# Spectra of the later rows as full-precision products instead of split ones, in a fused decoder-layer kernel

## The reference, cut to what matters

```
x = x + autocorrelation(Q = layernorm(x), K = ctx, V = ctx)

qf, kf = fft(q), fft(k)                      # over the 128 tokens, for each feature
corr   = ifft(qf * conj(kf)).real
w, idx = top_k(corr over the tokens, 9 of 128)
w      = softmax(w)
out    = sum over i of w_i * v shifted by idx_i   (positions clamped at the last token)
```

## Time and profile before

| | before |
|---|---|
| median of 3 runs | 1228.88 us (1228.21 to 1229.78) |
| profiled execution | 1230.26 us, span 1228.4 us |
| TensorE busy | 1022.5 us (83%) |
| VectorE busy | 929.4 us (76%) |
| ScalarE busy | 610.1 us (50%) |
| GpSimd busy | 486.6 us (40%) |
| mean granted TensorE clock | 0.927 |

### The profile page before, as it was taken

How to read it: one execution, slowest core, us unless ns; L and a number is a source line. 1 busy time by engine, 2 the same in 40 slices (tenths; PEclk the granted TensorE clock), 3 DMA queues, 4 the chain that set the end, 5 groups by cost and what they waited for, 6 DMA issues and landing times. The chain is left out here.

```text
span 1228.4 us, 23475 instructions
## 1 busy us (share of the span) xinstructions
PE 1022.5 (83%) x7936; PEld 776.0 (63%) x7936; DVE 929.4 (76%) x2818; ACT 610.1 (50%) x1803; POOL 486.6 (40%) x676
## 2 busy tenths in 40 slices
PE   5699999999999999999657999999898787615056
PEld 4577777877777777777445677777666564313034
DVE  6766786666787666776604878879999999997994
ACT  6434555444555544555515667777565564212023
POOL 2523433333443333443313766666565563101020
PEclk9799999999999999999778999999999998857579
DMA  9011011111011111011122222422332211139025
GB/s 378 29 42 51 25 58 58 58 47 51 17 58 58 58 58 41 28 47 42 47 100 86 86 91 74 129 91 78 91 106 74 75 56 39 43 116 343 0 52 137
DMA packets 47234, 95.71 MB, mean 78 GB/s; under 512 B 5952, under 2 KB 30400, under 8 KB 47168
## 3 DMA queue, kind: packets, MB, share of 16 engines
q1 hardware_dynamic: 47168, 94.91, 23.1%
HBM read 64.48 MB, written 27.26 MB: 75 GB/s over the span
## 5 line engine op out<-in xcount | busy, mean ns | idle before, releaser
L614 POOL TENSOR_TENSOR prob_G<-prob_G,rl 128x512 f32<-128x512 f32 x96 | 100.0, 1042 | 257.3 <-DVE rl L502 257.3
L384 ACT ACTIVATE prob_G<-prob_G,negm 128x128 f32<-128x128 f32 x384 | 148.9, 390 | 88.8 <-DVE negm L444 88.8
L244 PE MATMUL ps_qkv<-w_hi,xT_hi 128*128 128x512 f32 x384 | 156.6, 408 | 12.5 <-DVE prob_G L507 8.5
L245 PE MATMUL ps_qkv<-w_lo,xT_hi 128*128 128x512 f32 x384 | 151.6, 395 | 0.0
L246 PE MATMUL ps_qkv<-w_hi,xT_lo 128*128 128x512 f32 x384 | 151.2, 394 | 0.0
L316 PE MATMUL ps_qkv<-wo_hi,aT_hi 128*128 128x512 f32 x256 | 108.0, 422 | 0.0
L318 PE MATMUL ps_qkv<-wo_hi,aT_lo 128*128 128x512 f32 x256 | 102.3, 399 | 0.0
L317 PE MATMUL ps_qkv<-wo_lo,aT_hi 128*128 128x512 f32 x256 | 102.1, 399 | 0.0
L244 PEld LDWEIGHTS ps_qkv<-w_hi,xT_hi 128*128 128x128 f32 x384 | 73.1, 190 | 39.0 <-issue 17.0
L440 DVE TENSOR_TENSOR prob_G<-ps_s,mask 128x512 f32<-128x512 f32 x96 | 64.9, 676 | 41.0 <-PE ps_s L227 40.5
L469 DVE TENSOR_TENSOR xT_lo<-ps_t,xT_hi 128x512 fp32r<-128x512 f32 x16 | 11.1, 691 | 102.9 <-ACT xT_hi L423 102.9
(11 more groups left out here) (248 smaller groups left out, 2773.0 us busy)
## 6 DMA issues: line engine op xcount, KB each, us to landing
xin<-in_x SPq DMA_DIRECT2D x16, 512.0 KB, 3.3
xres<-in_x SPq DMA_DIRECT2D x16, 512.0 KB, 5.2
x<-xres SPq DMA_DIRECT2D x16, 512.0 KB, 2.6
c_xin<-x SPq DMA_DIRECT2D x16, 512.0 KB, 5.2
c_cin<-in_ctx SPq DMA_DIRECT2D x16, 512.0 KB, 4.5
c_b_xres<-x SPq DMA_DIRECT2D x16, 512.0 KB, 3.3
rows_x<-c_row SPq DMA_DIRECT2D x64, 128.0 KB, 2.3
m_xm<-rows_x SPq DMA_DIRECT2D x16, 512.0 KB, 8.6
```

Source lines behind the costliest of these rows:

```text
L244: nc.tensor.matmul(ps_qkv[:, n, :], xT_hi[:, k, :], w_hi[:, k, cols], start=k == 0, stop=False)
L245: nc.tensor.matmul(ps_qkv[:, n, :], xT_hi[:, k, :], w_lo[:, k, cols], start=False, stop=False)
L384: r = nc.scalar.activation(prob(g)[:, j, :], prob(g)[:, j, :], ACT.Exp, bias=negm[:, h:h + 1], accum_out=lsum[:, h:h + 1])
L614: nc.gpsimd.tensor_tensor(prob(g), prob(g), rl[:, g * GROUP:(g + 1) * GROUP].rearrange("p (j o) -> p j o", o=1).to_broadcast([P, GROUP, T] ...
```

## The change

For rows 9 to 15 (`whole(n)`: the tenth row on), the spectra are single float32 products of the unsplit row with the unsplit matrices. The copies to the high part and the subtractions for the low part aren't issued for these rows. The context of such a row is fetched straight into one of two buffers `c_whole`, which lie at the addresses of the two `c_lo` buffers; its DMA waits for the value spectra of row b in place of the splits of row b+1. TensorE waits for the landed context and for the normalised row in place of the splits. ScalarE's normalising of such a row waits for the query spectrum of the row before it, which reads the same tile `xn`. All sizes, tables of chain steps and other orders stay.

```diff
+        def whole(n):
+
+            return isinstance(n, int) and n >= 9
...
-                if ahead:
+                if ahead and whole(b + 2):
+                    sp.wait_ge(v_ps, 2 * (b + 1))
+                    sp.dma_start(c_whole[par][:], ctx_in[b + 2]).then_inc(cin_in, 16)
+                elif ahead:
                     sp.wait_ge(chi_done, b + 2)
                     sp.wait_ge(clo_done, b + 2)
                     sp.dma_start(cin[:], ctx_in[b + 2]).then_inc(cin_in, 16)
+                if ahead:
                     sp.wait_ge(xn_done, b + 2)
...
                     cols = slice(n * HALF, (n + 1) * HALF)
+                    if lo is None:
+                        r = nc.tensor.matmul(dst[:, n, :], mats[:, i, :], hi[:, cols], start=True, stop=True)
+                        continue
                     nc.tensor.matmul(dst[:, n, :], fwd_hi[:, i, :], hi[:, cols], start=True, stop=False)
                     nc.tensor.matmul(dst[:, n, :], fwd_hi[:, i, :], lo[:, cols], start=False, stop=False)
                     r = nc.tensor.matmul(dst[:, n, :], fwd_lo[:, i, :], hi[:, cols], start=False, stop=True)
...
+                of_context = (c_whole[1 - par], None) if whole(c) else (c_hi[1 - par], c_lo[1 - par])
                 if near:
-                    pe.wait_ge(xnh_done, c + 1)
-                    pe.wait_ge(xnl_done, c + 1)
+                    if whole(c):
+                        pe.wait_ge(xn_done, c + 1)
+                    else:
+                        pe.wait_ge(xnh_done, c + 1)
+                        pe.wait_ge(xnl_done, c + 1)
...
-                    split3(p_a, 0, xn_hi, xn_lo).then_inc(q_ps, 1)
+                    split3(p_a, 0, *((xn, None) if whole(c) else (xn_hi, xn_lo))).then_inc(q_ps, 1)
...
-                    pe.wait_ge(chi_done, c + 1)
-                    pe.wait_ge(clo_done, c + 1)
+                    if whole(c):
+                        pe.wait_ge(cin_in, 16 * (c + 1))
+                    else:
+                        pe.wait_ge(chi_done, c + 1)
+                        pe.wait_ge(clo_done, c + 1)
...
             def split_context(n, par):
+                if whole(n):
+                    return
                 act.wait_ge(cin_in, 16 * (n + 1))
...
-                if later(n, 0):
+                if whole(n):
+                    act.wait_ge(q_ps, n)
+                    act.wait_ge(xnl_done, 9)
+                elif later(n, 0):
                     act.wait_ge(xnl_done, n)
                 nc.scalar.activation(xn[:], xin[:], ACT.Identity, bias=norm2_v[:, turns(n, par), par, 1:2],
                                      scale=norm2_v[:, turns(n, par), par, 0:1]).then_inc(xn_done, 1)
+                if whole(n):
+                    return
```

More of the change, by code:

```diff
@@ L798, in autocorrelation_phase @@
         c_hi = [sb(f"c_hi{i}", [P, D], F32R) for i in range(2)]
-        c_lo = [sb(f"c_lo{i}", [P, D], F32R) for i in range(2)]
+        c_whole, c_lo = [], []
+        for i in range(2):
+            with ExitStack() as shared:
+                c_whole.append(shared.enter_context(nc.sbuf_tensor(f"c_c_whole{i}", [P, D], F32)))
+            c_lo.append(sb(f"c_lo{i}", [P, D], F32R))
         k_spec = [sb(f"k_spec{i}", [P, D]) for i in range(2)]
@@ L1042, in residual_taken @@
                             pe.wait_ge(x2_done, 2 * b + n - 1)
-                    split3(p_b, 0, c_hi[1 - par], c_lo[1 - par], residual_taken).then_inc(k_ps, 1)
+                    split3(p_b, 0, *of_context, residual_taken).then_inc(k_ps, 1)
                     if far:
                         pe.wait_ge(v_done, 2 * b + 2)
-                    split3(p_c, 1, c_hi[1 - par], c_lo[1 - par]).then_inc(k_ps, 1)
+                    split3(p_c, 1, *of_context).then_inc(k_ps, 1)
                 if far:
@@ L1089, in body @@
                     pe.wait_ge(corr_done, 2 * c + 2)
-                    split3(p_a, 2, c_hi[1 - par], c_lo[1 - par]).then_inc(v_ps, 1)
+                    split3(p_a, 2, *of_context).then_inc(v_ps, 1)
                     if far:
                         pe.wait_ge(tw_done, 4 * b + 4)
-                    split3(p_c, 3, c_hi[1 - par], c_lo[1 - par]).then_inc(v_ps, 1)
+                    split3(p_c, 3, *of_context).then_inc(v_ps, 1)
                 if far:
```

## The result

The changed kernel takes 1227.46 us (median of 12 runs, 1222.91 to 1228.57) against 1229.97 us (median of 12, 1228.21 to 1230.62): ratio 0.9976, interval 0.9965 to 0.9986, about 2.5 us faster by the medians and 3 us by the ratio. A gain was forecast, 3.5 us to 1225.4 us, range 1222.8 to 1229.4. The range holds the time. The gain came out 0.5 to 1 us smaller; another 1.1 us of the distance to 1225.4 is the starting point, since the forecast counted from the 1228.88 us of three runs and the twelve have 1229.97. The spread is 5.7 us against 2.4 us in these runs, but later sets of 15 to 24 runs of the kernel before spread over 3.8 to 6.3 us.

The account below looks back on a forecast made before the run. VectorE was taken to bound the spectral loop from body 8 on, TensorE body 7. Bodies 8, 9, 10 with 11, 12 and 13 gave 0 + 1.3 + 0.9 + 0.7 + 0.6 = 3.5 us less: 1225.4 us, range 1222.8 to 1229.4.

Parts of the forecast that it names:

- VectorE's stalls: Bodies 8 to 13: 19 chain products on VectorE wait out GpSimd's splitting pieces; removing these saves 3.36 us.
- The clock: Heads of bodies 9 and 10: less TensorE idle time ends the falls to half clock, saving 0.8 and 0.6 us.
- Body 8: Spectral-loop body entered by TensorE without pause: second VectorE product 0.7 us later cancels 0.67 us of stalls, so 0.
- TensorE's floor: Bodies 8 to 13: TensorE's path of 23.9 plus 1.6 us lets none take less than 25.5 us.
- the prediction's own sign of being wrong: VectorE waiting for weights' spectra or correlations in bodies 12 to 14, clock falls at new places, or a body below 25.5 us.
- Body 7: Spectral-loop body where TensorE sets the end: loses about 1 us of VectorE stalls, but gains nothing.
- The gain is carried to the end: Behind body 14: a VectorE chain with a fixed list of steps, so the 3.5 us gain reaches the end.
- TensorE in VectorE's place: Rival, every body's head: key spectra, weights' spectra, correlations reach VectorE 0.5 us later; about -1 us, 1227.9 us; chance 0.13.
- Falls that stay: Rival, bodies 9 and 10: clock falls remain where they are; gain only 1.8 us, 1227.1 us; chance 0.12.
- A fall at the head of every body: Rival: five more bodies and the two old ones have clock falls; +4.0 us, 1232.9 us; chance 0.08.
- Stalls that merely move to GpSimd's sums: Rival: chain steps shift against GpSimd's sums, nothing changes on the path; within 1 us of 1228.9; chance 0.11.
- The rate by the Trainium skill: Per 512-column half: skill pages give 0.65 against 0.86 us, +0.22 us; floor 26.1 us, sum about -1.1 us; trace's +0.16 us preferred.

Follow-up runs that it names:

- the three traces of the changed kernel's pipeline: Changed kernel traced twice (1227.46 and 1227.18 us), and once with ten overwritten TensorE products added at the start of the mixing phase (1223.99 us).
- The second trace of the kernel before: The kernel before run once more, nothing changed: 1232.78 us in a single run.
- without splitting: Against the changed kernel: rows 9 to 15 stay three split products, fed with parts left over from earlier rows, without any splitting; 1227.78 us, ratio 0.9976.
- products alone: Against the kernel before: all splitting kept, rows 9 to 15 use single float32 products of the high part with unsplit matrices; 1229.82 us, ratio 1.0003.
- filler: Ten overwritten 256-column float32 TensorE products at the start of the mixing phase: 1223.99 us in the changed kernel, 1227.64 us in the one before.

## Why the prediction was right, point by point

The cause it named is the one the runs show: without GpSimd's splitting pieces VectorE's chain loses the stalls beside them, and the two runs without these pieces gain as much as the whole change. That the time came out as near as it did is in part luck. The bodies gave 4.7 us, not 3.5, as the terms of the sum were off in both directions, and the medians kept only 2.5 to 3 us of that.

**VectorE's stalls.** Right in mechanism and size. 3.36 us were counted instruction by instruction over 19 chain products; a count of every one that overlaps a splitting piece gives 21 and 3.7 us, and 3.8 us went. The two runs without GpSimd's subtractions show 0.34, 0.69 and 0.72 us in bodies 11 to 13 against 0.30, 0.68 and 0.70, and 0.67 us in body 8 once TensorE doesn't stand in the way. Of ScalarE's copies nothing counted, as forecast, in bodies 8 to 14.

**The clock.** Right in direction, for a reason that is only in part borne out. No fall stands in bodies 8 to 13 in any of the three traces of the changed kernel's pipeline, and VectorE's waits for key spectra are left in body 8 alone (1.7 and 0.2 us):

```profile
DVE c_tq L1327 <- ACT c_k_spec L1175: 1.9, 2, 1.7
```

But they were taken for a fixed property of bodies 9 and 10. The second trace of the kernel before has them in bodies 9, 11 and 13. The change takes away idle time: TensorE waits 0.35 us ahead of body 9's first half and 1.17 between its halves, in place of 2.03 and 1.34.

```profile
873.56 1.10 PE L992 MATMUL pair<-c_c_whole,c_mats 128*128 128x512 f32 x2 [0.35 <-DVE c_x L1316]
875.83 1.12 PE L992 MATMUL pair<-c_c_whole,c_mats 128*128 128x512 f32 x2 [1.17 <-DVE c_x L1316]
```

That this is why the falls went fits body 9 in every trace, but it is not shown as a rule. Ahead of body 13 TensorE is idle 2.6 us in the first and third traces of the kernel before and 2.0 us in the three of the changed one, and no fall follows. Body 10 lost its fall without splitting too, where the products and 1.1 us of idle time ahead of it stayed.

**Body 8.** The term was 0.7 us against 0.67, so 0; measured -0.38 without splitting and +0.89 for products alone, together +0.51 (changed kernel: +0.52). Bodies 7 and 8 have to be read together. Without splitting body 7 is 0.33 us shorter as well, in sum 0.71 against the 0.67 counted. VectorE is through with body 7 earlier, but TensorE enters body 8 without a pause, so VectorE waits longer for its first key spectrum (before, then without splitting):

```profile
849.56 1.22 DVE L1298 TENSOR_TENSOR c_tq<-pair,c_k_spec 128x1024 f32<-128x1024 f32 x1 [0.42 <-ACT c_k_spec L1146]
850.29 1.22 DVE L1326 TENSOR_TENSOR c_tq<-pair,c_k_spec 128x1024 f32<-128x1024 f32 x1 [1.03 <-ACT c_k_spec L1174]
```

So the stalls were sized rightly, and the six halves cost 0.9 us, not 0.7. Both bodies together take 0.2 us more than before, and the term was short by that.

**TensorE's floor.** Wrong in size, and by the prediction's own sign of being wrong (a body below 25.5 us). Bodies 10 and 11 were to take 25.5 us each at least; they take 25.34 and 24.83, and bodies 9 and 13 take 25.42 and 25.34. That there is a floor is right: from body 11 to body 12 the changed TensorE no longer idles. From its first key half to that of the next body it takes 24.99 us, against 25.30 with 1.26 idle at the end before:

```profile
927.05 0.47 PE L979 MATMUL pair<-c_c_hi,c_fwd_hi 128*128 128x512 f32 x1 [1.41 <-DVE c_x L1287]
928.01 0.50 PE L979 MATMUL pair<-c_c_hi,c_fwd_hi 128*128 128x512 f32 x1
```

```profile
925.62 3.80 PE L992 MATMUL pair<-c_c_whole,c_mats 128*128 128x512 f32 x8 [0.19 <-DVE c_x L1316]
950.61 1.94 PE L992 MATMUL pair<-c_c_whole,c_mats 128*128 128x512 f32 x4
```

So of +1.6 us in ten halves 0.95 to 1.1 us showed, the higher figure when the idle time is taken from the spacing of starts (1.41 us) instead of the modelled end. Two idle times had been counted as TensorE's own path. It waited 1.12 us for ScalarE to take out the weights and waits 0.82 now. And its second key half starts 0.96 us after the first before (an unhindered one 0.70) and 0.97 us after it now, as it waits for the residual's second half in any case, so the first half's +0.16 us was free. 1.6 - 0.30 - 0.16 = 1.14 us. Bodies 10 and 11 together gave 1.7 us, where VectorE's own sum was 1.4 and the floor left 0.9.

**Body 7.** 0 forecast, -0.3 measured (23.20 to 22.89 us, also with no splitting): it belongs to body 8's stalls, as said above.

**The gain is carried to the end.** This step did not hold in size: the pipeline gave 4.7 us, the medians 2.5 to 3 (the interval reaches from 1.7 to 4.3). "The work behind is a VectorE chain with a fixed list of steps" overlooked that this chain waits 6.6 to 9.5 us for ScalarE, which waits for products that TensorE makes after an idle stretch, at 0.5 of the clock for a time that differs between executions by up to 7 us. But that adds scatter and isn't shown to eat gain. Every trace's span falls into four parts: up to the first fetch of the pipeline (658.6 to 661.9 us), the bodies, the end of the pipeline (59.3 us in all fourteen), and the mixing phase. Without its filler the last took 132.2 to 133.9 us in the five traces of the kernel before and its variants and 131.2 to 134.3 us in the six of the changed one and its variants, on average 133.3 and 133.0. So no part behind or ahead of the bodies is seen to lose what they gain, and why the medians show 1.7 to 2.2 us less stays open. The slowest runs have no trace.

**The rivals.** TensorE in VectorE's place: bodies 11, 12 and 14 of the products alone exclude it, and with the stalls gone bodies 10 to 13 are even 0.04 to 0.07 us shorter in the changed kernel than without splitting. Falls that stay: none is left in bodies 8 to 13 in the three traces of the changed pipeline. A fall at the head of every body: none came there either; single ones beside full-precision halves cost 0, 0.8 and 1.7 us in the other runs, so it would have taken three or more to undo 4.7 us. Stalls that merely move to GpSimd's sums: the 80 products lost 3.8 us in all.

**The rate by the Trainium skill.** The Trainium skill, "TensorE: Matmul & The Clock Gate", section "Back-to-back issue gap", gives about 216 ns for a pass of 512 columns, and "FP8 and Floating Point Precision", section "TensorE Precision Notes", four passes for true fp32; the estimate from both was +0.22 us a half and a gain of 1.1 us. In the traces the single product agrees with it: its half takes 0.86 us. The split one doesn't: 0.70 us, not 0.65. The difference is 0.16 us a half, so the trace's rate was the one to use.

## What to carry to other kernels

A GpSimd instruction can cost a two-input instruction of VectorE on SBUF a stall of half its own length and more (0.66 us in place of 0.26 beside pieces of 0.7 us), even when GpSimd itself is idle for four tenths of the body: count it on VectorE's path. Fewer but longer TensorE products can be free where another engine sets the time, and they fill idle time after which the clock may fall; they begin to cost in the body that TensorE enters without idle time, so place the switch one body later. When a gain in one phase is to reach the end, look at every wait in the later phases: a stretch there that begins at half clock can move the end by as much as the gain itself, and a few products into PSUM that is overwritten anyway shorten it.

## What the runs showed of the hardware

The return of the clock in a phase that TensorE starts cold came between 16.1 and 22.9 us after the phase began, in executions of the same program that agree in the 430 us ahead within 0.1 us, and moved the end by 3 us. With the ten products in place, TensorE busy 7.4 us of the first 13 in place of 2.0, it came after 8.7 to 11.5 us. Within the pipeline the clock's falls are not repeatable: three traces of one and the same stretch have them in bodies 9 and 10, in 9, 11 and 13, and in 9 and 10, at a cost of 0 to 1.8 us each.
